# Gapped rows for the fp8 steps, and one element per partition in VectorE's small operations

## What is computed

```python
x = x + L0_xattn(layernorm(x), ctx)   # one head, energies from ctx alone
x = x + L0_ffn(layernorm(x))          # rms norm, 8-bit activations, ternary weights
x = x + L1_xattn(layernorm(x), ctx)   # 16 heads of 128, 8 key/value heads
x = x + L1_ffn(layernorm(x))          # weights through fp8:

def _quantized_matmul(x, w, scale):
    wq = w.astype(jnp.float8_e4m3fn).astype(x.dtype)
    return jnp.einsum('bsi,io->bso', x, wq) * scale

# in L0_ffn, before each of its two products:
scale = 127 / jnp.maximum(jnp.max(jnp.abs(h), axis=-1, keepdims=True), 1e-5)
q = jnp.clip(jnp.round(h * scale), -128, 127) / scale
```

## Time and profile before

| | |
|---|---|
| median of 3 runs | 313.3 us (310.11 to 313.8) |
| the profiled execution | 312.58 us |
| its span, first to last instruction | 310.5 us |
| instructions | 6396 |
| mean granted TensorE clock | 0.995 |

### The profile page before, as it was taken

One profiled execution on the slowest core, in us unless ns is written; L12 is line 12 of the kernel. 1 busy time (PEld: TensorE's weight loads), 2 busy tenths in 40 slices (PEclk: granted clock), 3 DMA queues, 4 the chain that ended last, 5 costly groups with the idle time before them and its releaser, 6 DMA issues.

```text
span 310.5 us, 6396 instructions
## 1 busy us (share of the span) xinstructions
PE 293.6 (95%) x1980; PEld 259.9 (84%) x1992; DVE 260.9 (84%) x713; ACT 253.7 (82%) x603; POOL 218.5 (70%) x290
## 2 busy tenths in 40 slices
PE   3968999999999999999999999999999999999994
PEld 2755487798989998979889999999988999899884
DVE  3959999999999999889999986997768897675665
ACT  2398995598999998979999899778899999855460
POOL 3558864556998578999879998886678798952001
PEclk9979999999999999999999999999999999999999
DMA  7996032001326548885878756537645647200103
GB/s 223 367 381 199 35 101 70 1 8 30 93 47 189 157 138 251 220 212 139 228 210 226 199 144 174 161 108 219 182 144 148 179 143 211 68 3 0 36 1 101
DMA packets 54609, 44.59 MB, mean 144 GB/s; under 512 B 11696, under 2 KB 45104, under 8 KB 54576
## 3 DMA queue, kind: packets, MB, share of 16 engines
q1 hardware_dynamic: 54016, 43.93, 49.0%
q10 hardware_dynamic: 560, 0.26, 0.3%
HBM read 27.01 MB, written 15.20 MB: 136 GB/s over the span
## 4 chain that ended last, share of the span: by engine, by line
PE 59%; DVE 20%; DMA 8%; issue 5%; SPq 4%; ACT 2%; DVEq 0%
PE pb L2016 41%; DMA block_room<-blocks 5%; PE pb L2279 5%; PE pb L2314 4%; DMA wraw<-in_wgvT 3%; DVE blocks L1581 3%; SPq L442 2%; DVE sm L1564 2%; PE pb L2130 2%; PE pb L2091 2%; PE pb L2076 2%; DVE wraw L1455 2%; DVE step L1601 1%; PE pb L2227 1%; DVE q_lo L1551 1%
## 5 line engine op out<-in xcount | busy, mean ns | idle before, releaser
L667 POOL TENSOR_TENSOR tp_lo<-tp,pT_hi 128x512 fp32r<-128x512 f32 x54 | 70.0, 1311 | 15.1 <-ACT pT_hi L993 14.8
L981 ACT ACTIVATE sm<-sm,smin 128x256 f32<-128x256 f32 x128 | 63.6, 501 | 4.7 <-DVE smin L1564 4.4
L1564 DVE CUSTOM_DVE_ANT_0 sm<-pb,mask_all 128x256 f32<-128x256 f32 x128 | 47.3, 418 | 5.6 <-PE pb L2016 5.5
L1581 DVE STREAM_TRANSPOSE blocks<-sm 128x1024 f32<-128x1024 f32 x27 | 33.5, 1240 | 7.4 <-DMA block_room<-blocks 7.0
L2016 PE MATMUL pb<-ctx_hi,q_hi 128*128 128x256 f32 x128 | 38.1, 298 | 1.1 <-DVE q_lo L1551 0.6
L662 POOL TENSOR_SCALAR sm<-sm,srec 128x256 f32<-128x256 f32 x64 | 30.5, 488 | 10.4 <-DVE srec L1570 10.4
L2016 PE MATMUL pb<-xT_hi,m_hi 128*128 128x256 f32 x128 | 37.3, 292 | 0.3 <-DVE xT_lo L1540 0.3
L2016 PE MATMUL pb<-n_hi,oT_hi 128*128 128x256 f32 x128 | 37.1, 290 | 0.2 <-DVE oT_lo L1595 0.2
L2016 PE MATMUL pb<-xT_hi,m_lo 128*128 128x256 f32 x128 | 36.2, 283 | 0.0
L2016 PE MATMUL pb<-xT_lo,m_hi 128*128 128x256 f32 x128 | 36.2, 283 | 0.0
L2016 PE MATMUL pb<-ctx_lo,q_hi 128*128 128x256 f32 x128 | 36.2, 282 | 0.0
(11 more groups left out here) (195 smaller groups left out, 943.0 us busy)
## 6 DMA issues: line engine op xcount, KB each, us to landing
block_room<-blocks SPq DMA_DIRECT2D x108, 128.0 KB, 2.8
tp<-block_room SPq DMA_DIRECT2D x54, 256.0 KB, 3.0
w_raw<-in_w SPq DMA_DIRECT2D x4, 576.0 KB, 4.6
wraw<-in_wgvT SPq DMA_DIRECT2D x4, 512.0 KB, 8.4
wraw<-in_woutT SPq DMA_DIRECT2D x2, 512.0 KB, 9.3
out<-xb SPq DMA_DIRECT2D x4, 256.0 KB, 2.2
xa<-in_x SPq DMA_DIRECT2D x3, 256.0 KB, 4.5
xb<-in_ctxT SPq DMA_DIRECT2D x2, 256.0 KB, 5.1
```

Source lines behind the costliest of these rows:

```text
L667: g.tensor_tensor(tp_lo[:, z, c, :], tp[:, z, c, :], as_f32(pT_hi[:, c, :]), ALU.subtract).then_inc(pT_lo_pool, 1)
L981: a.activation(sm[:, n % 2, k, :], sm[:, n % 2, k, :], ACT.Exp, bias=smin[:, n % 2, k:k + 1], scale=-1.0, accum_out=ssum[:, n % 2, k:k + 1 ...
L1564: v.tensor_tensor_reduce(out=sm[:, n % 2, k, :], in0=bank(passing_bank("s", 2 * n + h))[:, (k % 2) * S:(k % 2 + 1) * S], in1=mask_all[:, b ...
L1581: v.transpose(blocks[:].rearrange("p g k b -> p k g b"), sm[:, n % 2, :, :].rearrange("p k (g b) -> p k g b", b=32)).then_inc(blocks_done, 1)
```

## The change

`sum8` becomes a tile of three rows of 96 elements at a pitch of 97, and all operations of a piece see it and its partners as three rows of 96. VectorE's exponent now goes to `sum8` and from there to `step8`, where it was made in place. In the statistics and in `scaled`, an instruction over two tiles becomes two instructions over one; the products of two [P, 2] tensors become products by a pointer operand [P, 1]. hmax and its lower bound move into one instruction, and hstep is then a product by 1/127 alone. The reciprocal stays one instruction over two tiles. No list of calls is changed.

```diff
--- before.py
+++ after.py
@@ -97,7 +97,7 @@
         cr_lo = tile(ctx, "cr_lo", [P, B * SC, P], F32R)
         xn = tile(ctx, "xn", [P, 2, TB, D])
         step8 = tile(ctx, "step8", [P, PIECE])[:]
-        sum8 = tile(ctx, "sum8", [P, PIECE])[:]
+        sum8 = tile(ctx, "sum8", [P, 3, PIECE // 3 + 1])[:, :, 0:PIECE // 3]
         identf = tile(ctx, "identf", [P, P])
         identb = tile(ctx, "identb", [P, P], BF16)
         mask_all = tile(ctx, "mask_all", [P, B, S + 1])
@@ -354,6 +354,9 @@
         def lows_before(n, c, pool):
             return sum(low_by_pool(m, d) == pool for m in range(n + 1) for d in range(SC) if (m, d) < (n, c))
 
+
+        def thirds(piece):
+            return piece.rearrange("p (a n) -> p a n", a=3)
 
         def some_key(b):
             return mask_all[:, b, S:S + 1]
@@ -667,17 +670,17 @@
                 g.tensor_tensor(tp_lo[:, z, c, :], tp[:, z, c, :], as_f32(pT_hi[:, c, :]), ALU.subtract).then_inc(pT_lo_pool, 1)
 
             def eighths(n):
-                raw = w8_raw[:, n * PIECE:(n + 1) * PIECE]
+                raw = thirds(w8_raw[:, n * PIECE:(n + 1) * PIECE])
                 pool.wait_ge(exp8_done, 2 * n + 2)
-                g.tensor_tensor(sum8, raw, step8, ALU.add).then_inc(sum8_done, 1)
+                g.tensor_tensor(sum8, raw, thirds(step8), ALU.add).then_inc(sum8_done, 1)
 
             def eighths_out(n):
                 pool.wait_ge(sum8_done, n + 1)
-                g.tensor_tensor(sum8, sum8, step8, ALU.subtract).then_inc(step8_done, 1)
+                g.tensor_tensor(sum8, sum8, thirds(step8), ALU.subtract).then_inc(step8_done, 1)
                 pool.wait_ge(step8_done, 2 * n + 1)
-                g.tensor_scalar(step8, sum8, FP8_OVER, 0.0, ALU.mult, ALU.mult).then_inc(step8_done, 1)
+                g.tensor_scalar(thirds(step8), sum8, FP8_OVER, 0.0, ALU.mult, ALU.mult).then_inc(step8_done, 1)
                 pool.wait_ge(step8_done, 2 * n + 2)
-                g.tensor_tensor(w8r[:, n * PIECE:(n + 1) * PIECE], sum8, step8, ALU.add).then_inc(w8_done, 1)
+                g.tensor_tensor(thirds(w8r[:, n * PIECE:(n + 1) * PIECE]), sum8, thirds(step8), ALU.add).then_inc(w8_done, 1)
 
             def rows4(b):
                 power(slice(0, 1), b, ve4_done, rstd4_done)
@@ -1407,10 +1410,13 @@
                 for t in range(sl.start, sl.stop):
                     v.bn_aggr(mv[:, t, :], bnst[:, t, :]).then_inc(mv_done, 1)
                 dve.wait_ge(mv_done, bn_count[0])
-                v.tensor_scalar(nmean[:, sl], mv[:, sl, 0], -1.0, None, ALU.mult)
+                for t in range(sl.start, sl.stop):
+                    v.tensor_scalar(nmean[:, t:t + 1], mv[:, t, 0:1], -1.0, None, ALU.mult)
 
             def variances(sl, done):
-                v.tensor_scalar(ve[:, 0, sl], mv[:, sl, 1], EPS, None, ALU.add).then_inc(done, 1)
+                for t in range(sl.start, sl.stop):
+                    ins = v.tensor_scalar(ve[:, 0, t:t + 1], mv[:, t, 1:2], EPS, None, ALU.add)
+                ins.then_inc(done, 1)
 
             def stats1(b):
                 dve.wait_ge(ld_x[b], 16)
@@ -1458,8 +1464,10 @@
                 sl = tiles(b)
                 dve.wait_ge(x1_done, b + 1)
                 stats(xa, sl)
-                v.tensor_scalar(ve[:, 0, sl], mv[:, sl, 1], EPS, None, ALU.add)
-                v.tensor_scalar(ve[:, 1, sl], mv[:, sl, 1], 1.0 + EPS, EPS * EPS, ALU.mult, ALU.add).then_inc(ve2_done, 1)
+                for t in range(sl.start, sl.stop):
+                    v.tensor_scalar(ve[:, 0, t:t + 1], mv[:, t, 1:2], EPS, None, ALU.add)
+                    ins = v.tensor_scalar(ve[:, 1, t:t + 1], mv[:, t, 1:2], 1.0 + EPS, EPS * EPS, ALU.mult, ALU.add)
+                ins.then_inc(ve2_done, 1)
 
             def centred(b):
                 dve.wait_ge(ve2_done, b + 1)
@@ -1477,22 +1485,34 @@
 
             scale_count = [0]
 
-            def scale_next(ins):
+            def scale_part(ins):
                 scale_count[0] += 1
                 ins.then_inc(scale_step, 1)
+
+            def scale_next(ins):
+                scale_part(ins)
                 dve.wait_ge(scale_step, scale_count[0])
 
             def scaled(b):
                 sl = tiles(b)
                 dve.wait_ge(gmax_done, b + 1)
                 dve.wait_ge(rstd2_done, b + 1)
-                scale_next(v.tensor_tensor(hmax[:, sl], hmax[:, sl], rstd[:, 1, sl], ALU.mult))
-                scale_next(v.tensor_scalar(hstep[:, sl], hmax[:, sl], EPS, 1.0 / 127.0, ALU.max, ALU.mult))
+                each = [slice(t, t + 1) for t in range(sl.start, sl.stop)]
+                for one in each:
+                    scale_part(v.tensor_scalar(hmax[:, one], hmax[:, one], rstd[:, 1, one], EPS, ALU.mult, ALU.max))
+                dve.wait_ge(scale_step, scale_count[0])
+                for one in each:
+                    scale_part(v.tensor_scalar(hstep[:, one], hmax[:, one], 1.0 / 127.0, None, ALU.mult))
+                dve.wait_ge(scale_step, scale_count[0])
                 scale_next(v.reciprocal(hrec[:, sl], hstep[:, sl]))
-                scale_next(v.tensor_tensor(hqs[:, sl], hrec[:, sl], rstd[:, 1, sl], ALU.mult))
+                for one in each:
+                    scale_part(v.tensor_scalar(hqs[:, one], hrec[:, one], rstd[:, 1, one], None, ALU.mult))
+                dve.wait_ge(scale_step, scale_count[0])
                 if b == 0:
                     dve.wait_ge(wmean_done, 1)
-                v.tensor_scalar(gsc[:, sl], hstep[:, sl], wmean[:, 0:1], None, ALU.mult).then_inc(gsc_done, 1)
+                for one in each:
+                    ins = v.tensor_scalar(gsc[:, one], hstep[:, one], wmean[:, 0:1], None, ALU.mult)
+                ins.then_inc(gsc_done, 1)
                 for t in range(TB):
                     tt = TB * b + t
                     ins = v.tensor_scalar(gbuf[:, b % 2, t, :], gbuf[:, b % 2, t, :], hqs[:, tt:tt + 1], ROUND, ALU.mult, ALU.add)
@@ -1598,10 +1618,10 @@
                 dve.wait_ge(ld_eight[n // B], 16)
                 if n >= 1:
                     dve.wait_ge(w8_done, n)
-                v.tensor_scalar(step8.bitcast(I32), w8_raw[:, n * PIECE:(n + 1) * PIECE].bitcast(I32), 0x7F800000, None,
+                v.tensor_scalar(sum8.bitcast(I32), thirds(w8_raw[:, n * PIECE:(n + 1) * PIECE]).bitcast(I32), 0x7F800000, None,
                                 ALU.bitwise_and).then_inc(exp8_done, 1)
                 dve.wait_ge(exp8_done, 2 * n + 1)
-                v.tensor_scalar(step8, step8, FP8_LEAST, FP8_STEP, ALU.max, ALU.mult).then_inc(exp8_done, 1)
+                v.tensor_scalar(thirds(step8), sum8, FP8_LEAST, FP8_STEP, ALU.max, ALU.mult).then_inc(exp8_done, 1)
 
             def added3(b):
                 dve.wait_ge(attn_ps, PAIRS * (b + 1))
```

## The result

The changed kernel takes 315.8 us (median of 11 runs, 312.9 to 318.8) against 313.2 us for the kernel before on the same chip: ratio 1.0087, 95% interval 1.0054 to 1.0121. Measured again on another occasion it gave 1.0043 (1.0011 to 1.0075). So it is slower by some 0.4 to 0.9%, 1.3 to 2.7 us, where 311.5 us was forecast, 0.6% faster than the median of before. It is within 2%, but outside the range and on the other side.

A forecast was written before the change was run, and what follows sets the result against it. The prediction took PE to bound the kernel. From the profiled execution, 312.6 - 1.8 + 0.0 = 310.8 us; as that execution lies 0.7 us under the median, the forecast was 311.5 us, range 308.3 to 314.8.

The forecast's parts named there:

- What bounds the kernel: Whole kernel: bound by PE, busy 95% of the span; from 62 us a faster VectorE gains only PE's waits.
- Part 1, the price of a step: Step operations on gapped rows: steady 0.44 us each, no collisions; 14.1 us against 21.7, VectorE losing 7.6 us of load.
- Part 1, the path: PE's pauses at about 121, 134 and 156 us go, plus some other idle time: -1.8 us, from -4.5 to 0.
- Part 1, GpSimd: GpSimd's four operations per piece on gapped rows: nothing added, upper end 1.3 us.
- Part 2: Small statistics and scaled operations: VectorE gains 4.5 us, loses 3.1 us of jumps; path term 0, between -1 and +1.5.
- No wait, semaphore or DMA is added: Gapped step operations: VectorE already waits for the previous piece's last GpSimd step before writing; no cost was added.
- A: Step operations: the shape changes nothing, they collide as before and only the small operations count; 313.3 us, chance 0.17.
- B: Transposed blocks' DMA round trip: PE's pauses reappear behind the transposes, a third of the 1.8 left; 312.7 us, chance 0.20.
- C: Early chain to 76 us: pointer operations cost full duration, no jump goes; 316.2 us, decides from 1.8 us early loss, chance 0.10.
- D: 62 to 241 us: GpSimd isn't held either, all PE idle time goes, hidden overlap included, 4.5 us; 308.8 us, chance 0.12.

The follow-up runs named there:

- e10: Gapped rows of the step operations alone, tiles behind sum8 moved by 512 bytes so the block tile is placed as in the kernel before; ratio 0.9914 to it.
- e9: Changed kernel with tiles behind sum8 moved by 512 bytes, so the block tile is placed as in the kernel before; ratio 0.9957 to the kernel before.
- e5: Changed kernel with sum8 lengthened so that the block tile begins at a multiple of 512 bytes; ratio 0.9953 to the kernel before.
- e6: Gapped rows alone, small operations as before, sum8 lengthened so the block tile begins at a multiple of 512 bytes; ratio 0.9922 to the kernel before.
- e0: The changed kernel once more, unaltered, timed beside the kernel before; ratio 1.0043.
- e1: Kernel before with the gapped rows of the step operations alone, small operations as before, block tile 32 bytes later; ratio 1.0028.
- e2: Kernel before with the small operations tile by tile alone, step operations as before; ratio 1.0003.
- e4: Kernel before with sum8 32 bytes longer, unused, so every tile behind it begins 32 bytes later; ratio 1.0102.
- e11: Kernel before with 32 bytes put in just ahead of the block tile, moving it and the three tiles behind; ratio 1.0070.
- e16: Kernel before with the block tile 32 bytes later, pT_lo unmoved and the two oT tiles moved by 128 bytes; ratio 1.0110.
- e3_nogap: Kernel before with the step operations cut in three rows that touch, no gap, small operations as before; ratio 0.9995.

## Why the prediction was wrong

**What bounds the kernel: right.** PE is busy for 95% of e10's span as of before's. The profile shows little of the gain as idle time, though: over the span PE's idle time is 310.5 - 293.6 = 16.9 us in before and 305.2 - 289.0 = 16.2 in e10. Most of the 5.3 us between the two spans lies in PE's drawn busy time, where by the prediction pauses hide in the overlap; how much of it is that, and how much that e10's was its fastest execution, isn't shown.

**Part 1, the price of a step: right.** Forecast 0.44 us, measured 0.438 and 0.453 as means; 7.0 + 7.2 = 14.2 us in all, where 14.1 were forecast for 21.7. Groups of VectorE by form, after:

```profile
L1621 DVE TENSOR_SCALAR sum<-w_raw 128x288 int32<-128x288 int32 x16 | 7.0, 438 | 0.7 <-POOL w8r L683 0.7
L1624 DVE TENSOR_SCALAR step<-sum 128x288 f32<-128x288 f32 x16 | 7.2, 453 | 0.6
```

**Part 1, the path: right in its mechanism, on the small side.** The term was -1.8 us (-4.5 to 0). The gapped rows by themselves at the old placement give 0.0086 x 312.3 = -2.7 us (-1.6 to -3.8 by the interval), 0.9 us more than the term. The stops at 121, 134 and 156 us are gone in after too, but others have come, such as this one:

```profile
130.82 0.38 PE L2036 MATMUL pb<-n_hi,oT_hi 128*128 128x256 f32 x1 [0.73 <-DVE oT_lo L1615]
```

In the trace of e10 PE has no stop of 0.1 us or more between 77 and 246 us.

**Part 1, GpSimd.** Forecast at nothing, up to +1.3 us. The like of L679 above (median 771 ns) in the kernel before:

```profile
L676 POOL TENSOR_TENSOR sum<-sum,step x16: 791/806/822, 93.5 to 271.8; 128x288 f32<-128x288 f32 x16
```

So gapped rows are no dearer there; GpSimd's busy time fell by 2.3 us.

**Part 2: right in load, a little too low on the path.** VectorE's busy time fell to 255.3 us, forecast about 255. The term was 0 (-1 to +1.5). Four pairs of kernels differ by the small operations alone: e9 less e10 +0.0043, e5 less e6 +0.0031, e0 less e1 +0.0015, e2 less before +0.0003. Their mean is 0.0023, 0.7 us. Each pair is uncertain by 0.3 to 0.5%, so between 0 and some 1.4 us is all that can be said. Of the chain: in `scaled(0)` from the first small step to the rounding 1.4 us instead of 0.96, which is the 0.5 of the forecast; in `scaled(1)` 1.43 instead of 1.68, since a jump of 0.75 has gone. At 76.21 PE still stands 0.29 us for pT_lo, where it was 0.48.

**The step that failed: "No wait, semaphore or DMA is added".** It is true, and the sum went on from it as if every line that isn't edited kept its price. The DMAs that were there, 108 writes from the block tile, land later, because the gap moves their source by 32 bytes. The diff shows it, in the shape `[P, 3, PIECE // 3 + 1]`. By the runs with the block tile at that very place the term is +0.7 to +1.1% in the kernel before (e4, e11 and e16, in the mean 0.94%, 2.9 us), and +0.9 to +1.3% in the changed ones (e0 and after against e9, e1 against e10), in all +2.2 to +4.1 us. With the terms measured, that of the place in the kernel before alone, the sum is -2.7 + 0.7 + 2.9 = +0.9 us, each term uncertain by about 1 us. The two measurements of the changed kernel gave +1.3 and +2.7, each to within 1 us: the first fits, the second lies at the edge of it. The sign is the term's: where the tiles stay at their places, the same change is faster (e9, 0.9957), and those 1.3 us of gain lie within the range of the prediction. The bounds of the range had no place for it, since no part had such a term.

**The rivals.** A (the shape changes nothing) is false: e1's steps are steady. What it feared of rows that touch is what e3_nogap shows: three rows that touch on both sides collide as one of 288 does. B saw the place where the loss would show, more idle time ahead of the transposition: 21.0 us in all in after. But it took that for the place to which PE's pauses would move once VectorE was faster, at a price of two thirds of the gain, 1.2 us. With the tile well placed the gain is there (e9, 0.9957), although the transposition waits for the blocks for 14.6 us. That idle time is no measure of the loss: it grows too when VectorE gets there sooner. Nor is PE's idle time between 62 and 241 us, 3.2 in e9 and 3.3 in after, nor most of the late stop behind `fuse`, of which e9 has 1.29 us:

```profile
238.80 0.36 PE L2036 MATMUL pb<-ctx_hi,q_hi 128*128 128x256 f32 x1 [1.29 <-DVE fuse L1649]
```

So B's wait is real at the good place too; what it costs there is inside e9's time. C, the slower one, has the right sign for a wrong reason: `scaled(0)` grew by 0.5 us, PE's progress in after is level with before's at 76 and 90 us to 0.1 us, and it needed 1.8. D, all idle time gone, is not reached even by e10, with 1.1 us left in its fastest execution.

**Two rules of the Trainium skill.** The exclusive lock ("SBUF — State Buffer", section "SBUF: two separate sides") agrees with all 32 steps at 409 to 455 ns once they are off the fast pace, although 30 of them run beside a GpSimd operation in after. By "Vector Engine (DVE) Microarchitecture Reference", section 5.1, the two-port mode needs the outermost dimension longer than one to be even in source and destination, or odd and as long in both; 288 against three rows would lose it, and the steady steps agree. An operation on one element per partition has no such dimension, so by these words the rule doesn't say what it does. Here none of the 104 one-element instances that the change brings in exceeds 215 ns, 56 of them beside a GpSimd operation.

## What to carry to other kernels

A changed tile size is a change to the address of every tile behind it. Before pricing an edit by its instructions, work out where the tiles behind it that DMAs read begin, and keep them where they were (here at a multiple of 128 bytes), or measure the old kernel with the new layout alone. If the edited lines do what they should and the time goes the other way, look at the durations of lines nobody touched, DMA landings first.

## What the runs showed of the hardware

- 512-byte DMA packets out of SBUF took 29.3 to 29.7 ns in the mean when their source began at a multiple of 256 bytes, 31.6 to 32.2 at 32, 64 or 128 past one, and 33.4 to 35.8 at 160 to 224 past.
- Four writes of 128 KB, of such packets, landed 0.1 to 0.5 us later per turn with the source off a multiple of 128 bytes, with packets no longer at 32 past; one trace at a multiple of 128 (e3_nogap) landed as late. Moving this one tile of 4 KB per partition by 32 bytes cost 1.1% of the kernel's time (e16_blocks_only); the other places off a multiple of 128, where tiles around it moved along, 0.3 to 1.0%.
- A VectorE operation on one element per partition stayed at or under 215 ns in all 104 instances; with two elements single ones took 0.6 to 0.8 us longer than the fastest of their line. In hmax and hqs the second tensor became a pointer operand too, so there the two effects aren't parted.
